# Gather stage of a graph layer: two accumulators in PSUM, waits behind TensorE's branch, and edges outside a block left unfetched

## What is computed

```python
xp = (x @ W).reshape(N, H, C)            # N = 3125, H = 4, C = 256
e = leaky_relu(a_src[src] + a_dst[dst], 0.2)
ee = exp(e - m[dst])
msgs = xp[src] * alpha[:, :, None]       # alpha = ee / z[dst]
out = segment_sum(msgs, dst, num_segments=N)
```

## Time and profile before

| | us |
|---|---|
| Device time, median of 3 executions (lowest, highest) | 2423.86 (2421.53, 2426.31) |
| The profiled execution's own time | 2426.14 |
| Its span, first to last instruction | 2424.4 |
| TensorE busy over the span | 2000.9 (83%) |
| VectorE busy over the span | 1517.8 (63%) |

### The profile page before, as it was taken

How to read it: one execution, slowest core, us unless ns; L and a number is a source line. 1 busy time by engine, 2 the same in 40 slices (tenths; PEclk the granted TensorE clock), 3 DMA queues, 4 the chain that set the end, 5 groups by cost and what they waited for, 6 DMA issues and landing times. The chain is left out here.

```text
span 2424.4 us, 53856 instructions
## 1 busy us (share of the span) xinstructions
PE 2000.9 (83%) x14842; PEld 1337.6 (55%) x14843; DVE 1517.8 (63%) x4465; ACT 1116.3 (46%) x2399; POOL 715.9 (30%) x935
## 2 busy tenths in 40 slices
PE   2888897666669999999999477874599999999997
PEld 1455555444437888788887354552344454545553
DVE  3776674677776777777777577886644434434333
ACT  2333442111117878787887455553344434434332
POOL 0002000000006666666666110010233323333222
PEclk9899998655589999999999698997799999999999
DMA  3533345233009999999999455555365465555542
GB/s 131 174 102 113 106 131 148 84 136 128 15 9 351 361 345 360 349 345 359 347 355 349 168 177 189 179 184 203 133 232 212 165 248 213 194 189 180 166 161 78
DMA packets 141058, 489.15 MB, mean 202 GB/s; under 512 B 22449, under 2 KB 22659, under 8 KB 138829
## 3 DMA queue, kind: packets, MB, share of 16 engines
q0 software_dynamic: 98912, 346.99, 41.1%
q1 hardware_dynamic: 41853, 140.70, 16.1%
q10 hardware_dynamic: 216, 0.43, 0.0%
HBM read 418.06 MB, written 81.27 MB: 206 GB/s over the span
## 5 line engine op out<-in xcount | busy, mean ns | idle before, releaser
L1035 PE MATMUL main_ps<-rows,O 128*128 128x256 f16 x4992 | 576.5, 273 | 49.1 <-DVE acc L974 28.6
L1021 ACT ACTIVATE O<-O,pk 128x128 f16<-128x128 f16 x1664 | 499.1, 387 | 126.0 <-DVE O L991 124.7
L1035 PEld LDWEIGHTS main_ps<-rows,O 128*128 128x128 f16 x4992 | 463.6, 98 | 119.8 <-DVE acc L974 33.7
L960 POOL DMA_INDIRECT rows<-projected,idx x416 | 394.7, 949 | 201.2 <-issue 89.7
L1755 PE MATMUL pj_ps<-gram,xsT 128*125 128x512 f16 x1200 | 293.3, 405 | 45.7 <-ACT xsT L396 45.1
L995 DVE TENSOR_SCALAR O<-O,pk 128x128 f16<-128x128 f16 x1664 | 318.8, 268 | 14.9 <-DVE O L991 0.2
L1706 PE MATMUL x_h<-w_p,gram 128*128 x1344 | 305.4, 385 | 15.2 <-ACT gram L1659 10.1
L1721 PE MATMUL x_o<-w_p,gram 128*128 x1344 | 308.0, 379 | 1.4 <-ACT gram L1675 1.4
L1755 PEld LDWEIGHTS pj_ps<-gram,xsT 128*125 128x125 f16 x1200 | 170.8, 146 | 156.3 <-ACT xsT L396 53.3
L1706 PEld LDWEIGHTS x_h<-w_p,gram 128*128 128x128 f16 x1344 | 131.3, 99 | 166.6 <-issue 25.7
L1764 PE MATMUL n_pj<-gram,PK 128*128 128x512 f16 (+3 forms) x900 | 170.7, 349 | 60.0 <-ACT PK L1226 60.0
(11 more groups left out here) (336 smaller groups left out, 2670.9 us busy)
## 6 DMA issues: line engine op xcount, KB each, us to landing
w_f<-in_L_ffn_W_dram SPq DMA_DIRECT2D x14, 2048.0 KB, 13.8
b_t<-in_L_ffn_b_dram SPq DMA_DIRECT2D x56, 512.0 KB, 3.7
xt<-in_x_dram SPq DMA_DIRECT2D x25, 500.0 KB
projected_f<-xp_f POOLq DMA_DIRECT2D x25, 500.0 KB, 3.7
projected<-xp POOLq DMA_DIRECT2D x25, 500.0 KB, 4.7
n_own<-projected_f SPq DMA_DIRECT2D x25, 500.0 KB
n_xt<-in_x_dram SPq DMA_DIRECT2D x25, 500.0 KB
out_dram<-n_x POOLq DMA_DIRECT2D x25, 500.0 KB, 9.9
```

The costliest lines, as they stand in the source:

```text
L960: pool.indirect_dma_start(out=rows[:, 4 * p + k, :, :].rearrange("k n d -> k (n d)"), out_offset=None, in_=xp_d[:, :], in_offset=bass.Indi ...
L1021: ins = act.activation(O[:, k, 1 + HEADS + h, :], O[:, k, 0, :], ACT.Copy, scale=pk[:, p, k, w:w + 1])
L1035: pe.matmul(main_ps[:, h * C:(h + 1) * C], O[:, k, 1 + HEADS * a + h, :], rows[:, 4 * p + k, b, h * C:(h + 1) * C], start=first and h % 2 ...
```

## The change

- `main_ps` and `small_ps` become two each, and block b uses number b mod 2 (`bank`). No matmul starts an accumulation group any more (`start=False` throughout): VectorE writes zeros to a pair after it has emptied it (`clear`: 1,024 columns of `main_ps`, 96 of `small_ps`), and to both at the start of the stage.
- TensorE's two arms are now one for each accumulator, and all waits stand inside the arm. Each arm waits on `s_seen` for the block's number plus one.
- `O` has eight slots; six are its own and two lie in unused parts of `gram`. VectorE waits for the visit eight back before it overwrites one. It looks at the flags of the two visits six and seven back. Its copy `pk16` moves from the start of the group to behind the second visit, with a wait of its own.
- GpSimd's loop and the copy to `idx` go: 416 indirect DMAs are written out, each with a bounds check. In an earlier stage three VectorE instructions of 408 columns add 4096 to the source index of every edge outside the visit's block (except in the first eight visits), so that the row is out of bounds and is not fetched.

The core of the diff, added lines (what is not shown declares or renames):

```diff
+RING, LAG, FAR = 8, 6, 4096
...
+    def bank(u):
+        return ((w >> (BITS * u)) & 1).with_bounds(min_val=0, max_val=1)
+
+    def emptied(u):
+
+        return (((w >> (BITS * u)) & ((1 << BITS) - 1)) + 1).with_bounds(min_val=1, max_val=BLOCKS)
+    return block, flag, bank, emptied
...
+                        off, later = mT[:, RING:VISITS, 0], slice(RING, VISITS)
+                        link(dve.tensor_scalar(off, dlocT[:, later], 0.0, None, ALU.is_lt))
+                        link(dve.scalar_tensor_tensor(off, dlocT[:, later], float(ROWS), off, ALU.is_ge, ALU.add))
+                        link(dve.scalar_tensor_tensor(srcT[:, later], off, float(FAR), srcT[:, later], ALU.mult, ALU.add))
...
+            own_slots = sbuf(c, "O", [P, RING - 2, 1 + 2 * HEADS, P], F16)
+
+            def O(n, w):
+
+                if n < RING - 2:
+                    return own_slots[:, n, w, :]
+                i, k = (KD - 1, w) if w < KD - 1 else (KD - 2, w - KD + 1)
+                return gram[:, n - RING + 2, i, k * P:(k + 1) * P]
             pk = sbuf(c, "pk", [P, 2, 4, PACK])
...
+            zero = sbuf(c, "zero", [P, 1])
+            main_ps = psum(c, "main_ps", [P, 2, D])
+            small_ps = psum(c, "small_ps", [P, 2, 512])
+            s_done, s_pk, s_seen, s_take = sem("ms_done"), sem("ms_pk"), sem("ms_seen"), sem("ms_take")
...
+                    bound = nc.alloc_register(mybir.EngineType.Pool, "last_node")
+                    pool.reg_mov(bound, NODES - 1)
+                    for v in range(VISITS):
+                        k = v % RING
+                        if v >= RING:
+                            wait_apart(pool, s_met, s_done, v - RING + 1)
+                        pool.indirect_dma_start(
+                            out=rows[:, k, :, :].rearrange("k n d -> k (n d)"), out_offset=None, in_=xp_d[:, :],
+                            in_offset=bass.IndirectOffsetOnAxis(ap=srcT[:, v:v + 1], axis=0),
+                            bounds_check=bound, oob_is_err=False).then_inc(s_row[k], 16)
...
+                    def clear(bank):
+                        dve.tensor_copy(of_bank(main_ps, bank), zero[:, :].broadcast_to([P, D]))
+                        dve.tensor_copy(of_bank(small_ps, bank)[:, 0:WIDE], zero[:, :].broadcast_to([P, WIDE])).then_inc(s_seen, 1)
...
+                    def take(b, bank):
+
+                        for n in range(2):
+                            half = slice(n * 512, (n + 1) * 512)
+                            a = acc[:, b, half] if isinstance(b, int) else acc[:, bass.ds(b, 1), half].squeeze(1)
+                            dve.tensor_copy(a, of_bank(main_ps, bank)[0:ROWS, half])
+                        dve.tensor_copy(at(sacc, b), of_bank(small_ps, bank)[0:ROWS, 0:2 * SUMS]).then_inc(s_take, 1)
...
+                    def takes(us, done, flags):
+
+                        block_at, last_at, bank_at, _ = flags
+                        with dve.If(last_at(us[0]) + last_at(us[1]) > 0):
+                            for n, u in enumerate(us):
+                                wait_apart(dve, s_met, s_done, done + n)
+                                with dve.If(last_at(u) == 1):
+                                    take(block_at(u), bank_at(u))
+                                    wait_apart(dve, s_met, s_take, done + n)
+                                    clear(bank_at(u))
+                                with dve.Else():
+                                    dve.nop().then_inc(s_take, 1)
+                        with dve.Else():
+                            dve.nop().then_inc(s_take, 2)
...
+                            wait_apart(dve, s_met, s_lo, 4 * (i - 1))
+                        dve.tensor_copy(pk[:, p, :, :], PK[:, sl, :]).then_inc(s_pk, 1)
+                        if not early(i, 1):
+                            flags = visit_word(dve, words, 1, i - 1)
+                        dve.wait_ge(s_pk, i + 2)
+                            v, n = 4 * i + k, 4 * p + k
+                                dve.wait_ge(s_done, v - RING + 1)
+                            dve.tensor_scalar(O(n, 0), iota16[:, :], pk[:, p, k, 0:1], None,
+                                ins = dve.tensor_scalar(O(n, 1 + h), O(n, 0), pk[:, p, k, 1 + h:2 + h],
+                            if k == 1:
+                                if not early(i, 2):
+                                    wait_apart(dve, s_met, s_done, 4 * (i - 1))
+                                dve.tensor_copy(pk16[:, p, :, 0:PACK], PK[:, sl, :]).then_inc(s_hi, 1)
+                            if k % 2 == 1 and not early(v, LAG + 1):
+                                takes((k - 1, k), v - LAG, flags)
+                    dve.memset(zero[:, :], 0.0).then_inc(s_pk, 1)
+                    dve.wait_ge(s_pk, 1)
+                    clear(0)
+                    clear(1)
+                    dve.memset(pk16[:, :, :, PACK:], 0.0)
...
+                    def products(i, j, p, k, bank, emptied):
+                        n = 4 * p + k
+                        pe.wait_ge(s_seen, emptied)
+                        pe.wait_ge(s_hi, 5 * i + (3, 3, 4, 5)[k])
+                        pe.wait_ge(s_lo, 4 * i + k + 1)
+                        pe.wait_ge(s_row[n], 16 * (j + 1))
+                                pe.matmul(main_ps[:, bank, h * C:(h + 1) * C], O(n, 1 + HEADS * a + h),
+                                          rows[:, n, b, h * C:(h + 1) * C], start=False, stop=True, skip_group_check=True)
+                        pe.matmul(small_ps[:, bank, 0:WIDE], O(n, 0), pk16[:, p, k, 1:1 + WIDE],
+                                  start=False, stop=True, skip_group_check=True).then_inc(s_done, 1)
+                        _, _, bank_at, emptied_at = visit_word(pe, words, 0, i)
+                            with pe.If(bank_at(k) == 1):
+                                products(i, j, p, k, 1, emptied_at(k))
+                                products(i, j, p, k, 0, emptied_at(k))
```

More of the change, by code:

```diff
@@ L136, in flag, with of_bank @@
         return (w >> (4 * BITS + u)) & 1
-    return block, flag
+    def bank(u):
[3 more added lines that the diff above has]
+    return block, flag, bank, emptied
+def of_bank(t, bank):
+    return t[:, bank, :] if isinstance(bank, int) else t[:, bass.ds(bank, 1), :].squeeze(1)
 class Wider:
@@ new lines, in _ @@
+                @block.vector
+                def _(dve):
+                    def clear(bank):
[20 more added lines that the diff above has]
+                            dve.nop().then_inc(s_take, 2)
@@ L994, in body @@
                             for h in range(HEADS):
[L995 removed]
+                                ins = dve.tensor_scalar(O(n, 1 + h), O(n, 0), pk[:, p, k, 1 + h:2 + h],
                                                         None, ALU.mult)
                             ins.then_inc(s_hi, 1)
[L999 to L1008 removed]
+                            if k == 1:
[9 more added lines that the diff above has]
+                    dve.memset(pk16[:, :, :, PACK:], 0.0)
                     steps(dve, GROUPS, body)
+                    flags = visit_word(dve, words, 1, GROUPS - 1)
+                    for k in (1, 3):
+                        takes((k - 1, k), VISITS + k - LAG, flags)
                     dve.wait_ge(s_done, VISITS)
[L1012 removed]
+                    take(BLOCKS - 1, (BLOCKS - 1) % 2)
                 @block.scalar
@@ L1033, in products @@
                             for a, b in ((0, 0), (0, 1), (1, 0)):
-                                pe.matmul(main_ps[:, h * C:(h + 1) * C], O[:, k, 1 + HEADS * a + h, :],
-                                          rows[:, 4 * p + k, b, h * C:(h + 1) * C],
-                                          start=first and h % 2 == 0 and a == b, stop=True, skip_group_check=True)
-                        if first and not early(v, 1):
-                            pe.wait_ge(s_seen, 3 * v)
-                        pe.matmul(small_ps[:, 0:WIDE], O[:, k, 0, :], pk16[:, p, k, 1:1 + WIDE],
-                                  start=first, stop=True, skip_group_check=True).then_inc(s_done, 1)
+                                pe.matmul(main_ps[:, bank, h * C:(h + 1) * C], O(n, 1 + HEADS * a + h),
+                                          rows[:, n, b, h * C:(h + 1) * C], start=False, stop=True, skip_group_check=True)
```

75 lines of the change are left out of this document (7 added, 68 removed).

## The result

The changed kernel takes 2427.88 us (median of 20 executions, 2423.29 to 2435.99), the kernel before beside it 2421.66 us (20, 2417.66 to 2427.28): a ratio of 1.0026, 95% interval 1.0019 to 1.0034. It is 0.26% or 6.2 us slower, where some 2.2 us less were forecast. The profiled execution took 2429.07 us, 2.9 more than that of the kernel before. The other 3.3 us are the scatter of single executions: the profiled one of the kernel before lay 4.5 us over its median, this one 1.2.

A forecast was written before the change was run, and what follows sets the result against it. TensorE and its accumulator hand-over bound the kernel; VectorE would next. Visits 548.6 plus boundaries 72.7 us, with the ends, made the stage 3.8 us shorter, less 1.6 earlier: net 2.2 us less, 2421.5 us, range 2394 to 2443.

The forecast's parts named there:

- What bounds the changed kernel: Gather stage: VectorE becomes the engine that sets the pace, 24.9 us a block against TensorE's 22.5 without stalls.
- the list of signs: Changed profile: no accumulator waits, TensorE waiting 2 to 3 us a block for matrices, VectorE some 90% busy, 13.3 MB less.
- What bounded the kernel before: Gather stage: TensorE and, 24 times, the hand-over of its one accumulator, 62.4 us idle; 61 us the most to gain.
- Eight visits: VectorE's pace in the stage: 10.2 us plus 0.17 a group for moved copy and waits, 10.55 us; 416 visits 548.6.
- The boundary: VectorE between blocks: copies, `sacc`, clearing and waits 3.24 us, less 0.2 hidden, 3.03 us, 24 times: 72.7 us.
- The end: Behind the last one-hot copy: TensorE's last visit 1.6 us and the last `take` 1.5, together 3.1 us.
- The start: Ahead of the first one-hot: two clearings 2.5 us, and the earlier stage's three VectorE instructions 1.6 us with waits.
- the point from which it decides: VectorE's time for a block from which the kernel becomes slower, 24.9 us; the sum all but touches it.
- VectorE is cheaper than summed: Rival, gather stage: waits cost nothing and clearing 0.6 us, 36 us under the sum, 2386 us; chance 0.17.
- The DMA engines set the pace: Rival, gather stage: transfers already bound the kernel before, so unfetched rows give 36 us, 2388 us; chance 0.05.
- VectorE is dearer: Rival, gather stage: 0.3 us a group and 3.9 a boundary, 35 us over the sum, 2456 us; chance 0.17.
- The instruction memory: Rival: VectorE's loop, 205 to 257 instructions, falls out of it, 50 us and up over 51 turns, 2475 us; chance 0.03.

The follow-up runs named there:

- run 1: The changed kernel without the clearing of main_ps at the block boundaries: 2422.99 us, ratio 0.9998 to the kernel before.
- run 4: The changed kernel with every slot fetched, without the three earlier instructions and the bound: 2424.93 us, ratio 1.0007 to the kernel before.
- Run 8: The kernel before with GpSimd's loop written out, indices read where they lie, no copy and no bound: 2421.97 us, ratio 0.9989.
- run 3: The kernel before with slots without an edge not fetched (three instructions ahead, a bound on the indirect transfer): 2435.38 us, ratio 1.0056.
- the early copy: Next group's fp32 copy `pk` made behind the third visit of the group ahead: changed kernel first 2493.06 us (0.9867), kernel before 2526.64 (1.0004).
- runs 1 to 4: run 1, run 3, run 4, and the changed kernel with a second clearing into spare PSUM at each boundary: 2455.31 us, ratio 1.0140.

## Why the prediction was wrong

**What bounds the changed kernel: right.** VectorE sets the pace over a block. A second clearing cost 27 us, 13.3 MB of transfers nothing, and TensorE's waits turned from the hand-over into 2 to 3 us a block for VectorE's and ScalarE's matrices, as the list of signs said. VectorE's busy share was forecast at some 90% and is 81% (469 of 580): the rest is gaps between its instructions, which I had put into the sum but not into the share.

**What bounded the kernel before: the engine was right, the price was not.** The prediction read the 62.4 us in 48 stretches as one sum, 2.6 us a boundary, with a second stop at the second half of `main_ps`. The tile's view adds up two rows of the same stop, the weight load (PEld) and the matmul (PE) behind it:

```profile
PEld main_ps L1035 <- DVE acc L974: 33.7, 24, 1.5
PE main_ps L1035 <- DVE acc L974: 28.6, 24, 1.3
...
1002.74 1.21 PEld L1035 LDWEIGHTS main_ps<-rows,O 128*128 128x128 f16 x12 [1.42 <-DVE acc L974]
```

Behind it the twelve matmuls run through. From the starts of the visits, the hand-over cost 32.6 us over TensorE's pace, 1.36 at each of 24 boundaries; 11.8 went at the other loop turns and 15.2 elsewhere, 59.6 in all. In the changed kernel the same count gives 0.1 at these places and 60.7 in all, now behind VectorE. So TensorE loses as much as before over the stage, but in stops of mostly 2 to 3 us once a block instead of 1.36, and the most that two accumulators alone could give was some 33 us and not 61. The forecast sum does not use this reading: it goes by VectorE.

**Eight visits, 10.55 us forecast, 10.64 measured: +4.6 us over 52 pairs.** The step that failed is "eight visits cost 10.2 us, 1.275 a visit", the base of the sum's largest term. It took the pace from undisturbed groups. Over the whole stage eight visits take 0.24 us more than the quickest in the changed kernel (10.64 to 10.40), and 10.45 against 10.11 in the kernel before, where I could have read it, with some waits in it. Against 10.45 the base was 13 us too low over 52 pairs. The price of the moved copy and the waits was not too low but too high: quickest to quickest 10.11 became 10.40, 0.15 us a group where 0.17 was forecast, and mean to mean only 0.1 a group, which took 8 us back. What makes the mean dearer than the quickest stays open in part. The trace of the changed kernel shows one piece: 168 of the 2,080 one-hots and scaled copies took over 0.35 us, the median being 0.25. Each of the 168 ran beside an indirect transfer's instruction on GpSimd, and none of the 413 that ran clear of one was among them; no run tests this.

**The boundary, 3.03 us forecast, 2.96 measured: -1.7 us, and right by two errors.** The clearing is 1,228 ns on the timeline (forecast 1.15 of 0.6 to 1.23) but worth 0.39 us on the path (run 1). I had 0.2 us hidden in the whole boundary; about 0.8 of the clearing alone is. What I left out is about as large: 0.65 us on average, not 0.55, ahead of the first copy, and the head of the next group, which no copy covered. That the sum came out is luck.

**The end, 3.1 us forecast, 5.5 measured: +2.4.** The sum let TensorE stand one visit behind VectorE. It starts its last visit 3.6 us after the last one-hot (1353.32 against 1349.75), so behind VectorE's last scaled copy three visits, 4.1 us, and the `take`, 1.4, follow.

**The start, 4.1 us forecast, 5.4 measured: +1.3.** The three instructions take 0.75, 0.91 and 0.88 us on 408 columns, not 0.5: 2.3 us of delay at the scans behind them and 2.6 at the stage, where 1.6 was forecast. The clearings cost 2.8 us against 2.5.

In the stage 4.6 - 1.7 + 2.4 and -0.1 of rest make the 5.2 us between the forecast -6.3 (net of the start) and the measured -1.1; with +1.3 at the start and -1.3 behind the stage, where I had nothing, the profiled execution is some 5 us over its forecast; the other 3.3 between forecast and medians are the scatter named above. So the forecast gain of 2.2 us was smaller than the error of its terms. The mechanism held and the sizes added up on one side; the text said that its sum all but touched the point from which it decides.

**The rivals.** *VectorE is cheaper than summed* (2386 us): half of its reason fits run 1, where instructions seem to queue up behind long copies, but most of the clearing's time came back as gaps. *The DMA engines set the pace* fell with run 4. *VectorE is dearer* had its own reasons (0.3 us a group, 3.9 a boundary), and neither came. *The instruction memory* did not matter: in the window only one instruction queue moves anything,

```profile
q14 instruction: 6, 0.05, 0.0%
```

one piece about every 96 us. Run 8, with VectorE's old loop and GpSimd's written-out program, shows the same six pieces, and the kernel before none, so they are GpSimd's; VectorE's loop of 257 instructions waited for none. The Trainium skill (Runtime: NRT & Kernel Launch, Instruction fetch mechanics) gives pages of 256 instructions and a window of two. By that, an estimate, 257 instructions in a row lie in two pages at most, and not in three as the prediction had it; the trace, without a fetch for them, agrees. The edit costed at nothing that was not nothing is the bound on the indirect transfer: 0.05 us each, free under the changed GpSimd loop and 11 us in the old one (run 3).

## What to carry to other kernels

Take an engine's pace from the mean of its groups over the stage, and use the quickest only to price an edit. Before adding up a tile's waits, look whether two engines' rows tell of the same stop. On an engine with short instructions do not read the gaps between them as room: here one long copy at a boundary was nearly free and a second one of the same length cost all of it, and taking a copy away was worth less than its duration as long as the registers, waits and branches beside it stayed. When two accumulators free the matmul engine, ask first how much faster than its pace the engine is that feeds it; here VectorE's 1.33 against TensorE's 1.353 us a visit let no lead build up that could cover 3 us at a boundary.

## What was not expected of the hardware

Two sets of runs, on chips recorded under the numbers 3 and 8, took 2527 us for the kernel before instead of 2422, all of it in the gather stage (732.9 us in the kernel before with the early copy, whose first one-hot stands at 723.8 us, against 723.4 in the kernel before at 2426). A chip numbered 8 is also recorded for runs 1 to 4, at 2422 us, so it is not shown that this belongs to a chip. The changed kernel took 2494 us there, 1.4% less than the kernel before. Its stage's window, and TensorE's timeline in the first run of the changed kernel with the early copy:

```profile
760.00:1340.00 580.00, 504.26 (x4561) 420.62 (x4559) 430.33 (x2021) 419.50 (x1392) 347.96 (x351) 1.00 0.88 298
```

```profile
917.04 0.20 PE L1082 MATMUL small_ps<-pk,O 128*128 128x96 f16 x1 [0.81 <-issue]
917.76 0.27 PE L1080 MATMUL main_ps<-rows,O 128*128 128x256 f16 x1 [0.51 <-issue]
918.49 1.72 PE L1080 MATMUL main_ps<-rows,O 128*128 128x256 f16 x11 [0.46 <-issue]
```

TensorE stops for 0.5 us in the middle of a visit, where its program has no wait. The window's granted clock is 1.00 in the changed kernel, so the clock is not what lengthens its stage. What does, and why the changed kernel suffers less from it, stays open; no run here separates it.

A row that is out of bounds was not fetched, as forecast: the stage moved 204.84 MB against 218.13, 13.3 less (191.50 against 204.45 in the window, at a DMA share of 0.92 where 0.96 stood).
